# Spare rows, early gathers, one mask on ScalarE and one clearing of semaphores in a one-core graph kernel

## The reference, cut to what matters

```python
# x: 100000 x 128 node rows; 50000 edges (src, dst, type), sorted by dst
h = relu(layernorm(x))
W = einsum('rb,bio->rio', w_comp, weight)          # 16 relations out of 8 bases
x = x + segment_sum((h @ W)[etypes, src], dst) + h_bias
h = leaky(relu(layernorm(x)) @ enc_w + enc_b)      # slope 0.1
for l in range(2):
    agg = segment_sum(h[src], dst) / max(degree, 1)
    h = leaky(agg @ lin_l_w[l] + lin_l_b[l] + h @ lin_r_w[l])
x = x + h
```

## Time and profile before

| what | before |
|---|---|
| median of three runs | 3398.31 us |
| the profiled execution's own time | 3396.55 us |
| its span, first to last instruction | 3394.8 us |
| busy: PE / DVE / ACT / POOL | 2463.2 / 2900.7 / 1885.4 / 2461.0 us |
| granted clock of PE, mean | 0.905 |
| DMA | 969.06 MB, mean 285 GB/s |

### The profile page before, as it was taken

How to read it: one execution, slowest core, us unless ns; L and a number is a source line. 1 busy time by engine, 2 the same in 40 slices (tenths; PEclk the granted TensorE clock), 3 DMA queues, 4 the chain that set the end, 5 groups by cost and what they waited for, 6 DMA issues and landing times. The chain is left out here.

```text
span 3394.8 us, 49738 instructions
## 1 busy us (share of the span) xinstructions
PE 2463.2 (73%) x13942; PEld 1823.4 (54%) x13942; DVE 2900.7 (85%) x8116; ACT 1885.4 (56%) x4895; POOL 2461.0 (72%) x2412
## 2 busy tenths in 40 slices
PE   2999999999999588888888888657777746663000
PEld 2555555555555366666666666557777735553000
DVE  4899888888888599999999999689999978776567
ACT  1566666666666498888888888635555521110000
POOL 4477777777777477777777777577777757778871
PEclk9999999999999799999999999979999978776555
DMA  9989888887222599999999999479999989999999
GB/s 244 371 325 283 260 235 257 239 258 227 77 82 73 185 282 283 286 284 283 287 284 283 285 285 282 125 254 340 341 333 346 312 314 416 416 416 404 399 407 357
DMA packets 642447, 969.06 MB, mean 285 GB/s; under 512 B 70661, under 2 KB 412295, under 8 KB 630370
## 3 DMA queue, kind: packets, MB, share of 16 engines
q1 hardware_dynamic: 532598, 717.70, 62.9%
q0 software_dynamic: 85376, 194.22, 17.8%
q10 hardware_dynamic: 24198, 53.96, 4.7%
HBM read 509.25 MB, written 464.73 MB: 287 GB/s over the span
## 5 line engine op out<-in xcount | busy, mean ns | idle before, releaser
L972 PE MATMUL y_ps_rel<-w_basis,ht_rel 128*128 128x512 f32 x1568 | 754.3, 605 | 4.0 <-DVE two_rel L831 4.0
L709 POOL DMA_INDIRECT agg<-rows_rel,put_c x392 | 408.0, 1041 | 160.9 <-issue 96.1
L1251 ACT ACTIVATE h_node<-base_node,shift_node,rstd_node 128x128 f32<-128x128 f32 x1176 | 500.3, 483 | 1.6 <-DVE shift_node L1331 1.6
L368 POOL DMA_INDIRECT gat_rel<-in_x_dram,src_c x392 | 406.8, 1038 | 125.1 <-issue 109.9
L1111 POOL DMA_INDIRECT base_and_means<-rows_node,odd_c x392 | 388.1, 990 | 145.9 <-issue 118.0
L1102 POOL DMA_INDIRECT term_node<-agg,src_c x392 | 394.1, 1005 | 132.7 <-issue 119.6
L1792 POOL DMA_INDIRECT gat_l<-base_and_means,src_c x392 | 393.5, 1004 | 119.7 <-issue 119.4
L831 DVE SCALAR_TENSOR_TENSOR two_rel<-y_ps_rel,coef,two_rel 128x128 f32<-128x128 f32 x1568 | 438.4, 343 | 0.0
L972 PEld LDWEIGHTS y_ps_rel<-w_basis,ht_rel 128*128 128x128 f32 x1568 | 273.9, 195 | 199.2 <-issue 138.0
L984 PEld LDWEIGHTS sum_ps_rel<-same_rel,two_rel 128*128 128x128 f32 x1568 | 238.5, 192 | 191.0 <-issue 188.2
L912 ACT ACTIVATE part_rel<-y_ps_rel,coef 128x128 f32<-128x128 f32 x784 | 242.4, 361 | 159.2 <-PE y_ps_rel L972 158.7
(11 more groups left out here) (216 smaller groups left out, 6408.7 us busy)
## 6 DMA issues: line engine op xcount, KB each, us to landing
pairs_l<-base_and_means SPq DMA_DIRECT2D x112, 512.0 KB
base_and_means<-zero_row SPq DMA_DIRECT2D x49, 1024.0 KB
means<-zero_row SPq DMA_DIRECT2D x49, 1024.0 KB, 10.9
first_node<-in_x_dram SPq DMA_DIRECT2D x196, 256.0 KB, 4.1
term_node<-agg SPq DMA_DIRECT2D x196, 256.0 KB, 4.6
x<-base_node SPq DMA_DIRECT2D x196, 256.0 KB, 4.6
base_and_means<-done_node SPq DMA_DIRECT2D x196, 256.0 KB, 4.4
out_dram<-last_z_l SPq DMA_DIRECT2D x98, 512.0 KB, 10.2
```

The costliest lines, as they stand in the source:

```text
L368: nc.gpsimd.indirect_dma_start(gat_rel[:, m % X_RING, j, :], None, x, bass.IndirectOffsetOnAxis(ap=src_c[:, m * HALF + j:m * HALF + j + 1] ...
L709: nc.gpsimd.indirect_dma_start(agg, bass.IndirectOffsetOnAxis(ap=put_c[:, t:t + 1], axis=0), rows[:, m % KEPT, j, :], None).then_inc(s_sca ...
L972: nc.tensor.matmul(y_ps[(q + j) % 2][:, c * 512:(c + 1) * 512], ht[:, q, j, :], w_basis[:, 4 * c:4 * c + 4, :], start=True, stop=True).the ...
L1251: last = nc.scalar.activation(h[:, n % 2, j * P:(j + 1) * P], base[:, n % SLOTS, j * P:(j + 1) * P], ACT.Relu, bias=shift[:, b % 2, c:c + ...
```

## The change

Four edits:

- AHEAD goes from 4 to 6, so POOL gathers 42 instead of 28 tiles in the preparation, and none in the relational stage before the first scatter's half step.
- The spare rows of `agg` are zeroed in SP's half step 0 instead of 2, those of `pair` in half step 10 (FILL_STEPS). The first scatter waits for the former alone; the latter have a semaphore of their own, for which SP waits at the end of the stage.
- In layer 1 `open_` is made by ACT (Relu of 1 - run number) instead of DVE, at the same place j = 3 of the half step. ACT waits for the run numbers and for DVE's last use of that buffer.
- The semaphores of the relational stage are not cleared behind it; they are cleared together with those of the joined pass. Code for l = 0 goes, with its 14 semaphores.

```diff
@@ -82,7 +82,7 @@
-    AHEAD = 4
+    AHEAD = 6
@@ -579,9 +579,12 @@
+        waiting = []
+
         def clear(held):
 
-            nc.clear_and_free_semaphores(held)
+            nc.clear_and_free_semaphores(waiting + held)
+            waiting.clear()
             nc.all_engine_barrier()
@@ -704,7 +707,7 @@
                             if m == 0 and j == 0:
-                                pool.wait_ge(s_spare, 2 * DMA)
+                                pool.wait_ge(s_spare, DMA)
@@ -749,11 +752,12 @@
                             spill(m)
-                            if m == 2:
+                            if m == 0:
                                 sp.dma_start(agg[N:N + SPARE, :].rearrange("(p j) f -> p j f", p=P),
                                              zero_row[:].unsqueeze(1).to_broadcast([P, SPARE // P, P])).then_inc(s_spare, DMA)
+                            if m == FILL_STEPS:
                                 sp.dma_start(pair[N:N + SPARE, :].rearrange("(p j) (k f) -> p (j k) f", p=P, f=P),
-                                             zero_row[:].unsqueeze(1).to_broadcast([P, SPARE // P * 2, P])).then_inc(s_spare, DMA)
+                                             zero_row[:].unsqueeze(1).to_broadcast([P, SPARE // P * 2, P])).then_inc(s_spare_pairs, DMA)
@@ -767,6 +771,7 @@
+                        sp.wait_ge(s_spare_pairs, DMA)
@@ -1006,7 +1011,7 @@
-            clear(held)
+            waiting.extend(held)
@@ -1871,11 +1871,6 @@
-                        def find_open(m, q):
-
-                            dve.wait_ge(s_runb[q], use(m, q))
-                            nc.vector.tensor_scalar(open_[:, q, :, :], columns(q), 0.0, None, ALU.is_equal).then_inc(s_open, 1)
-
@@ -1920,13 +1902,10 @@
-                                if more and j == 3:
-                                    find_open(m + 1, 1 - q)
@@ -1935,14 +1914,19 @@
+                        def find_open(m, q):
+
+                            act.wait_ge(s_runb[q], use(m, q))
+                            if m >= 2:
+                                act.wait_ge(s_carried, tile(m - 2, HALF - 1))
+                            nc.scalar.activation(open_[:, q, :, :], run_b[:, q, :].rearrange("p (t e) -> p t e", e=P),
+                                                 ACT.Relu, bias=ones[:, 0:1], scale=-1.0).then_inc(s_open, 1)
+
@@ -1960,8 +1944,11 @@
+                                if before(m, HALVES - 1) and j == 3:
+                                    find_open(m + 1, 1 - q)
                                 ago(m, q, i, j, 4, finish)
```

More of the change, by code:

```diff
@@ L1454, in layer_pass @@
                 s_gathered = [psem(f"gathered{g}") for g in range(RING)]
-                s_added = [[psem(f"added{q}{j}") for j in range(HALF)] for q in range(2)]
                 s_runb = [psem(f"run_b{q}") for q in range(2)]
@@ L1822, in put_late @@
                                 put(rows_, edges * HALF + j, s_late[q][j])
[L1824 to L1842 removed]
+                        for k in range(HALVES * HALF):
+                            gather(k // HALF, k % HALF)
                         if l:
@@ L1928, in _ @@
                         select(0, 0)
-                        find_open(0, 0)
                         count_needed(dve)
@@ L1937, in _ @@
                     def _(act):
+                        def find_open(m, q):
[4 more added lines that the diff above has]
+                                                 ACT.Relu, bias=ones[:, 0:1], scale=-1.0).then_inc(s_open, 1)
                         def finish(m, q, j):
                             act.wait_ge(s_rowed, tile(m, j))
[L1941 to L1945 removed]
+                            if m >= 2 and j == 0 and m < HALVES - KEPT:
+                                act.wait_ge(s_spilled[q], use(m - 2, q))
                             kept_at = m - (HALVES - KEPT)
```

26 lines of the change are left out of this document (2 added, 24 removed).

## The result

The change made the kernel slower: 3410.49 us (median of 7 runs, 3405.88 to 3413.45) against 3398.31 us (7 runs of the kernel before beside them), a ratio of 1.0034 [1.0023, 1.0046] (a third of a per cent, small but clear of the noise). 3364 us was forecast. The profiled execution of the changed kernel took 3413.45 us with a span of 3411.6 us, 16.8 us more than the span of before.

The account below looks back on a forecast made before the run. POOL was taken to bound the relational stage, with DVE and POOL nearly level in layer 1. The terms -18.0 - 1.3 - 14.6 = -33.9 us gave 3364 us on the scale of the median; range 3352 to 3384.

Parts of the forecast that it names:

- The bounds of the stages: Relational stage: POOL paces at 18.8 us a half step, first scatter held by `pair`'s zeros; layer 1: DVE and POOL nearly level.
- Part 1: Preparation: fourteen more gathers and POOL's drain start the relational stage at about 84.5 us, 7 us late; bounds 6 and 13.
- Part 2: Relational stage: first scatter at 108.9 instead of 127.87 us, same instructions at the same pace, so its end moves by -18.0 us.
- Part 3: Barrier before the joined pass: no clearing at 1145 us, -1.3 us; bounds 0.5 and 1.6.
- Part 4: Layer 1: with the mask off DVE, DVE starts on the last gather at 2714.0 instead of 2728.63 us, -14.6; bounds 5 and 21.
- some of the rest is L1890: Layer 1: DVE's mask L1890 stalls gathers overlapping it, 0.25 us at one of two half steps, 28 x 0.25 = 7 us.
- DVE's 30 us cover either: Layer 1: the 30 us of DVE freed by moving 56 masks suffice for a gain of either bound, 5 or 21 us.
- ACT's mask: Layer 1: the mask takes 0.95 us on ACT, hidden because PE waits for the next row only some 2.5 us later: 0.
- the fourth one: Rival, layer 1: ACT's mask enters the loop and PE waits for its rows; layer 38 us longer, total 3417; chance 0.05.
- The first: Rival, layer 1: DMA is next, faster pace pushes landings back; gain about 6 us instead of 14.6, total 3373; chance 0.15.
- The upper bound of 35 us of stalls: Layer 1: by the skill's lock rule 56 masks cost POOL up to 56 x 0.62 = 35 us; total gain 21 us.
- a layer whose half step is 8.9 us or longer: Layer 1: a sign named beforehand that would show the forecast wrong.

## Why the prediction was wrong

- **The bounds of the stages: right.** POOL paces the relational stage, and the zeros of `pair` held the first scatter. With them gone, it came at 109.11 us; 108.9 was forecast. The trace names a fill of `agg` as its releaser, but the first row ended at 108.29, and the scatter follows it by 0.82 us, just as in the kernel with the mask back on DVE, where the row itself is named (108.81 and 109.63): the row decided, as forecast.
- **Part 1, late start of 7 us: right in kind, 5.7 measured** (77.51 to 83.20). The last early gather ended at 77.06, as forecast (77.0); the DRAIN ended 5.8 us behind it, at 82.9, where 7.3 and 84.3 were forecast. That four early half steps beat six, by 4.5 us at the last scatter, follows from the step's own terms: the fifteen gathers left ahead of the first scatter, at 1.34 us each from 77.5, are done at 98, before the first row.
- **Part 2, -18.0: too large, -13.6 measured** at the end of the stage. The first scatter moved by 18.8 us, but from it to the last one it took 1010.4 us instead of 1005.3: the same 741 gathers and scatters were busy 4.8 us longer. I took "the same pace" for granted. Why they were slower is not shown; the rule found in layer 1 covers only about half of what these instructions take over their shortest.
- **Part 3, -1.3: right, -1.9 measured.** That is the time from barrier to barrier; the first gather comes 0.9 us behind the drain (1131.4 to 1132.28), before it was 2.3.
- **Part 4, -14.6: wrong in sign, +33.6 measured.** The step that failed is "some of the rest is L1890": I took the 1.19 us of the gather at 2707.68 for the mask's doing and let 28 such stalls of 0.25 us vanish with it. By the rule above that gather was held by the comparison L1883, which was running at its start, for 0.16 us, and by the mask for 0.1, so the masks cost some 2.4 us in the layer and not 7. And I took the stalls as a property of each operation, when they are one of the moment: the same add and leak that had cost the gathers 0.2 us in the whole layer cost them 21.6 (18.9 and 2.7), and the node rows' maximum 17.7 instead of 2.9, once DVE waited for landings. "DVE's 30 us cover either" was the error in a sentence: time freed on DVE was not neutral for POOL.
- **ACT's mask: 1.03 us instead of 0.95, hidden as forecast.** The kernels with the mask on neither and on both show that it costs nothing that can be seen.
- **The rivals.** The result is near the fourth one's 3417 us by number, but not by mechanism: PE waited for ACT's rows for 1.6 us in the whole layer. The first, that the transfers are next, has in common with what came that DVE waits for landings; but it allowed no loss, and what was late were POOL's own gathers. The upper bound of 35 us of stalls, worked out from the Trainium skill's rule, stood there as a possible gain; it came as a loss.
- **The signs named beforehand:** "a layer whose half step is 8.9 us or longer" is what came, 9.7 us in the mean. (It was loosely set: the steady half step of the kernel before is 8.96.)

The Trainium skill, in SBUF — State Buffer (Who interferes with whom), calls the shared port pair an exclusive lock that goes to whichever engine's instruction starts first. The trace agrees in one direction, once it is read gather by gather: what POOL pays is the rest of DVE's operation (0.58 us of 1.09 in the row at 2414.28). It doesn't agree in the other: a gather that started first doesn't hold DVE's add (1.08 to 1.09 us in either case) and is not held itself by one that reads two tensors and starts later. The prediction used the rule as a sum over 56 instructions, where the moment of each was what mattered.

What stays open: why the pattern of a DVE that paces the loop settles where the gathers start between its long operations, and that of a waiting DVE does not. The timelines suggest that a held gather ends soon after the operation that held it, and that POOL so falls in step, but no run took that alone.

## What to carry to other kernels

When POOL issues indirect transfers beside a DVE full of long operations that keep all their operands in SBUF, don't cost a relief of DVE by its own time alone: ask which of the two engines waits for the other afterwards. Here a DVE of 8.96 us a half step, 0.2 more than POOL's seven undisturbed gathers need (7 x 1.25), left POOL 1.00 us a gather, and one with less work than POOL made it 1.09 to 1.10; over 392 gathers that was more than all the work taken away. Try the cheap counter-check first: put the removed work back as idle work, and see if the time falls.

## What the runs showed of the hardware that was not expected

- An indirect gather on POOL takes 0.945 us; it is longer by the rest of a DVE operation with two SBUF inputs running at its start less 0.125 us, and by nothing for such a one that starts later (345 of 346 gathers to 0.04 us).
- A TENSOR_REDUCE over SBUF, 5.75 us long, held none of the four gathers that started inside it (0.945 to 0.949 us), and a gather already running held no add of DVE (1.08 to 1.09 us inside one and outside).
- 35 us of useless DVE work made the changed kernel 33 us faster (3410.49 to 3377.4; 1.0034 and 0.9928 of the kernel before beside each).
- The same operation in two pieces costs less to POOL (the add 18.9 and 8.3 us), but the next long one takes its place (2.7 and 13.9).
